# Two-layer transformer on one core: output normalisation of the second layer's attention once per batch instead of once per head group, room for a causal constant copied by ACT, and a new list of steps

## The reference

```python
A1 = where(causal, einsum('bhnd,bhmd->bhnm', Q1, K1) * scaling, -inf)
A2 = where(causal, einsum('bhnd,bhmd->bhnm', Q2, K2) * scaling, -inf)
attn = softmax(A1) - lam * softmax(A2)
O = einsum('bhnm,bhmd->bhnd', attn, V)
rms = sqrt(mean(O * O, axis=-1, keepdims=True) + EPS)
O = O / rms * rms_scale * (1.0 - LAMBDA_INIT)
```

## Time and profile before

| | |
|---|---|
| three runs, median | 509.58 us (508.74 to 510.84) |
| profiled execution | 509.87 us |
| its span | 507.8 us, 8609 instructions |
| PE busy | 462.9 us, 91% |
| DVE busy | 431.2 us, 85% |
| ACT, POOL busy | 265.4 us, 269.0 us |
| granted PE clock, mean | 0.979 |

### The profile page before, as it was taken

The page is one execution under the profiler, slowest core; times in us unless marked ns, Lnnn a source line. Parts: engine busy times, 40 slices in busy tenths (PEclk is TensorE's granted clock), DMA queues, the critical chain, the costliest instruction groups (busy, mean ns, idle before and its releaser), DMA issues.

```text
span 507.8 us, 8609 instructions
## 1 busy us (share of the span) xinstructions
PE 462.9 (91%) x3072; PEld 220.4 (43%) x3072; DVE 431.2 (85%) x812; ACT 265.4 (52%) x416; POOL 269.0 (53%) x229
## 2 busy tenths in 40 slices
PE   3998988999889999998899999999899899999986
PEld 2755444445344434454344444454434334433332
DVE  2735677798999999889979999979999999997894
ACT  1255553353676654346566654526775475357621
POOL 6311530364562558815645654814775759357962
PEclk9999997699999999999989999999999999999998
DMA  8800246926372521023067254121555135113100
GB/s 280 318 12 1 57 131 132 176 72 170 83 132 73 112 68 44 1 71 100 0 170 151 57 86 89 39 70 43 149 132 121 25 72 132 51 41 88 43 14 28
DMA packets 49889, 46.14 MB, mean 91 GB/s; under 512 B 6360, under 2 KB 39480, under 8 KB 49208
## 3 DMA queue, kind: packets, MB, share of 16 engines
q1 hardware_dynamic: 49848, 45.61, 35.8%
HBM read 37.47 MB, written 7.60 MB: 89 GB/s over the span
## 4 chain that ended last, share of the span: by engine, by line
PE 59%; DVE 27%; issue 5%; POOL 4%; ACT 2%; DMA 1%; SPq 1%; DVEq 0%; POOLq 0%; ACTq 0%
PE bank L779 8%; PE bank L791 6%; PE bank L770 6%; PE scores L810 6%; PE bank L865 4%; DVE h L1291 4%; DVE nmax L1315 4%; DVE h L1298 3%; PE scores L705 3%; PE scores L696 3%; PE scores L720 3%; PE scores L699 3%; PE scores L744 3%; PE scores L804 2%; DVE nmaxf L1315 2%
## 5 line engine op out<-in xcount | busy, mean ns | idle before, releaser
L1107 POOL TENSOR_TENSOR gb<-gb,wb 128x512 f32<-128x512 f32 x64 | 83.6, 1307 | 99.8 <-ACT gb L1006 83.9
L1021 ACT ACTIVATE pk<-scores 128x1024 f32<-128x1024 f32 x96 | 95.7, 1023 | 49.0 <-PE scores L810 48.6
L1100 POOL TENSOR_SCALAR_AFFINE_SELECT pk<-pk 128x512 f32<-128x512 f32 (+1 forms) x96 | 83.0, 871 | 54.1 <-ACT pk L1021 53.8
L1003 ACT ACTIVATE gt<-bank,bgh 128x512 f32<-128x512 f32 (+1 forms) x68 | 46.8, 688 | 75.5 <-PE bank L770 55.9
L1315 DVE TENSOR_REDUCE nmax<-scores 128x8 f32<-128x1024 f32 x64 | 76.8, 1214 | 6.5 <-PE scores L810 6.2
L779 PE MATMUL bank<-xnt,wu 128*128 128x512 f32 x128 | 70.0, 629 | 5.4 <-DVE h L1298 5.2
L770 PE MATMUL bank<-xnt,wg 128*128 128x512 f32 x128 | 70.2, 630 | 0.5 <-DVE hs L1298 0.3
L791 PE MATMUL bank<-h,wd 128*128 128x512 f32 x128 | 68.1, 628 | 0.6 <-DVE h L1298 0.5
L1298 DVE SCALAR_TENSOR_TENSOR h<-bank,bu,h 128x512 f32<-128x512 f32 x64 | 48.1, 751 | 10.1 <-PE bank L779 8.2
L1291 DVE SCALAR_TENSOR_TENSOR h<-gt,gb 128x512 f32<-128x512 f32 x64 | 52.1, 814 | 0.4 <-POOL gb L1107 0.4
L1111 POOL TENSOR_TENSOR orms<-oms,minus_half 128x32 f32<-128x32 f32 x8 | 43.8, 5481 | 7.8 <-DVE oms L1347 7.7
(11 more groups left out here) (258 smaller groups left out, 713.0 us busy)
## 6 DMA issues: line engine op xcount, KB each, us to landing
wb<-wt_scratch SPq DMA_DIRECT2D x64, 256.0 KB, 4.1
parts_scratch<-parts SPq DMA_DIRECT2D x48, 128.0 KB, 2.4
qa<-parts_scratch SPq DMA_DIRECT2D x32, 96.0 KB
ka<-parts_scratch SPq DMA_DIRECT2D x32, 96.0 KB
qa<-parts_scratch SPq DMA_DIRECT2D x32, 64.0 KB
ka<-parts_scratch SPq DMA_DIRECT2D x32, 64.0 KB
...
```

The costliest lines, as they stand in the source:

```text
L1003: A(gt[0:rows, c % 2, :], bank[5][0:rows, :], ACT.Tanh, bias=bgh[0:rows, j:j + 1], scale=0.5).then_inc(s_gate_act, 1)
L1021: A(dst.rearrange("p (h m) q -> p m h q", m=2), pairs[pair_of(step)][:, :, :].rearrange("p m (h q) -> p m h q", q=cols), ACT.Exp, scale=SC ...
L1100: pool.affine_select(out=dst, in_=dst, compare_op=ALU.is_ge, fill=0.0, base=0, pattern=[[0, heads], [1, P]], channel_multiplier=-1).then_i ...
L1107: pw(gb[:, c % 2, :], gb[:, c % 2, :], wb[:, k % 2, j % 2, :], ALU.mult).then_inc(s_ga_done, 1)
```

## The change

There are three parts.

1. A new kind of step, `seed`: for the units in `SEEDED`, ACT copies a 128x128 tile `late_f` (0 where the key may be seen, -1e30 elsewhere) into the eight parts of the room, and PE leaves out the mask matmuls and adds onto it. POOL makes the tile at the start, with one memset and one select. In `SEEDED` is a diagonal `max` unit if the taker two before it is of a kind in `("none",)`. The list has 64 `seed` words.
2. `back` keeps only the transpose, into one of four slots of `ot`. A new step `mix`, once for each batch, does the reciprocal, the product and the sum for all four groups; -lambda goes into the reciprocals of the second softmax first. The tiles `on` and `o12` go, `osq` and `lam_in` lie in `ot`, and the semaphore `oc_done` counts batches.
3. `PROGRAM` is a new list.

```diff
+    load/0 load/1 norm0/0 scale0/0 turn0/0 keys0/0 router0/0 inner0/0 norm0/1 picks0/0 scores0/0 hidden0/0 scale0/1
...
-N_MASKS = 10
+N_MASKS = 12
...
+SEEDED = [step for n, step in enumerate(TAKERS) if step[0] == "max" and step[4] < 2 and n >= 2 and TAKERS[n - 2][0] in ("none",)]
+SEED_RANK = {step: n for n, step in enumerate(SEEDED)}
...
-                                  start=(h == 0 and not masked), stop=True, skip_group_check=True)
+                                  start=(h == 0 and not masked and not seeded), stop=True, skip_group_check=True)
...
-                if kind in RING:
+                if step in SEED_RANK:
+                    pe.wait_ge(s_seed, SEED_RANK[step] + 1)
+                elif kind in RING:
                     ring_free(pe, step)
...
-                    last = scores(pair_of(step), b, query, P, qa, ka, MROWS, GH * g, key, P, u < 2)
+                    last = scores(pair_of(step), b, query, P, qa, ka, MROWS, GH * g, key, P, u < 2 and step not in SEED_RANK, step in SEED_RANK)
...
                 elif kind == "setup":
 
+                    act.wait_ge(s_masks_ready, N_MASKS)
...
+                elif kind == "seed" and ("max", c, *rest) in SEED_RANK:
+                    unit_step = ("max", c, *rest)
+                    ring_free(act, unit_step)
+                    A(pairs[pair_of(unit_step)][:, :, :].rearrange("p m (h c) -> p (m h) c", c=P),
+                      late_f[:, :].unsqueeze(1).to_broadcast([P, GHC, P]), ACT.Copy).then_inc(s_seed, 1)
...
                     dve.wait_ge(s_pv_ps, n + 1)
-                    V.transpose(ot[:, :, :].rearrange("p n r -> p (n r)"), bank[4]).then_inc(s_o_read, 1)
-                    dve.wait_ge(s_o_read, n + 1)
-                    link(V.reciprocal(rl1[:, :], ot[:, :, DV]))
-                    if n:
-                        dve.wait_ge(s_oc_done, n)
-                    link(V.tensor_tensor(o12[:, :, :], ot[:, :, 0:DV], wide(rl1[:, :], DV), ALU.mult))
-                    dst = oc[:, 2 * b:2 * b + 2, :].rearrange("p s (n r) -> p s n r", r=QUAD)[:, g // 2, :, g % 2 * DV:g % 2 * DV + DV]
-                    V.scalar_tensor_tensor(out=dst, in0=o12[:, BLOCKS:, :], scalar=lamq[:, g:g + 1], in1=o12[:, 0:BLOCKS, :],
-                                           op0=ALU.mult, op1=ALU.add).then_inc(s_oc_done, 1)
+                    if n >= MIX:
+                        dve.wait_ge(s_oc_done, n // MIX)
+                    V.transpose(ot[:, g % MIX, :, :].rearrange("p n r -> p (n r)"), bank[4]).then_inc(s_o_read, 1)
+                elif kind == "mix":
+                    b, m = rest
+                    n = group(c, b, m * MIX) // MIX
+                    dve.wait_ge(s_o_read, (n + 1) * MIX)
+                    link(V.reciprocal(rl1[:, :, :], ot[:, :, :, DV]))
+                    second = rl1[:, :, BLOCKS:]
+                    link(V.tensor_tensor(second, second, lamq[:, m * MIX:(m + 1) * MIX].unsqueeze(2).to_broadcast([P, MIX, BLOCKS]), ALU.mult))
+                    o = ot[:, :, :, 0:DV].rearrange("p m n d -> p (m n) d")
+                    link(V.tensor_tensor(o, o, wide(rl1[:, :, :].rearrange("p m n -> p (m n)"), DV), ALU.mult))
+                    both = ot[:, :, :, 0:DV].rearrange("p m (q n) d -> p m q n d", q=2)
+                    for a in range(MIX // 2):
+                        k = slice(2 * a, 2 * a + 2)
+                        dst = oc[:, 2 * b:2 * b + 2, :].rearrange("p s (n h d) -> p s h n d", h=2, d=DV)[:, (m * MIX) // 2 + a, :, :, :]
+                        ins = V.tensor_tensor(dst, both[:, k, 0, :, :], both[:, k, 1, :, :], ALU.add)
+                    ins.then_inc(s_oc_done, 1)
...
-                    dve.wait_ge(s_oc_done, group(c, b, GROUPS))
+                    dve.wait_ge(s_oc_done, group(c, b, GROUPS) // MIX)
```

More of the change, by code:

```diff
@@ L90 @@
[L90 to L109, removed]
@@ new lines @@
+    back/0/0/2 score/0/1/0/2 fetch/1/0 seed/1/0/0/0 up/12 scores0/2 gate/14 up/13 seed/1/0/0/1 max/1/0/0/0
+    seed/1/0/1/0 values/0/0/3 back/0/0/3 max/1/0/0/1 picks0/2 weights1/1 max/1/0/0/2 wb/8 seed/1/0/1/1 gate/15
+    max/1/0/1/0 score/0/1/1/0 values/0/1/0 mix/0/0/0 score/0/1/1/1 probs0/2 down/11 score/0/1/1/2 max/1/0/1/1 down/12
+    score/0/1/2/0 norm/0/0 back/0/1/0 score/0/1/2/1 down/13 score/0/1/2/2 up/14 max/1/0/1/2 values/0/1/1 seed/1/0/2/0
+    seed/1/0/2/1 max/1/0/2/0 gate/16 back/0/1/1 max/1/0/2/1 score/0/1/3/0 down/14 up/15 score/0/1/3/1 up/16
@@ new lines @@
+    score/0/1/3/2 seed/1/0/3/0 values/0/1/2 fetch/1/1 back/0/1/2 max/1/0/2/2 down/15 seed/1/0/3/1 max/1/0/3/0
+    values/0/1/3 back/0/1/3 max/1/0/3/1 max/1/0/3/2 mix/0/1/0 gate/17 down/16 seed/1/1/0/0 norm/0/1 seed/1/1/0/1
+    hidden0/2 seed/1/1/1/0 max/1/1/0/0 seed/1/1/1/1 gate/18 max/1/1/0/1 wb/9 seed/1/1/2/0 max/1/1/0/2 up/17 hidden1/2
+    minus/1/0 turn/0/0 wb/10 turn/0/1 up/18 values1/1 gate/19 max/1/1/1/0 max/1/1/1/1 out1/0 end/0 score/1/0/0/0
+    score/1/0/0/1 gate/20 max/1/1/1/2 down/17 fin/0 score/1/0/0/2 up/19 max/1/1/2/0 seed/1/1/2/1 out0/2 wb/11 up/20
@@ new lines @@
+    score/1/1/1/0 scale0/3 back/1/0/3 gate/24 seed/2/0/1/0 down/23 mix/1/0/0 store/2 up/24 score/1/1/1/1 score/1/1/1/2
+    gate/25 values/1/1/0 score/1/1/2/0 norm/1/0 fetch/2/0 router1/2 wb/13 back/1/1/0 down/24 turn0/3 up/25 max/2/0/0/0
+    max/2/0/0/1 gate/26 keys0/3 max/2/0/0/2 seed/2/0/1/1 max/2/0/1/0 up/26 gate/27 max/2/0/1/1 score/1/1/2/1 down/25
+    values/1/1/1 turn/1/0 max/2/0/1/2 score/1/1/2/2 down/26 gate/28 back/1/1/1 up/27 values/1/1/2 seed/2/0/2/0 wb/14
+    router0/3 score/1/1/3/0 max/2/0/2/0 up/28 score/1/1/3/1 gate/29 inner0/3 wb/15 score/1/1/3/2 seed/2/0/2/1 down/27
@@ new lines @@
+    max/2/0/2/1 max/2/0/2/2 gate/30 down/28 fetch/2/1 seed/2/0/3/0 seed/2/0/3/1 seed/2/1/0/0 seed/2/1/0/1 up/29
+    scores0/3 back/1/1/2 max/2/0/3/0 up/30 gate/31 values/1/1/3 max/2/0/3/1 max/2/0/3/2 back/1/1/3 choose1/2 down/29
+    up/31 picks0/3 gate/32 probs0/3 hidden0/3 hidden1/3 minus/2/0 mix/1/1/0 norm/1/1 max/2/1/0/0 max/2/1/0/1 up/32
+    gate/33 weights1/2 max/2/1/0/2 score/2/0/0/0 down/30 up/33 down/31 wb/16 turn/1/1 seed/2/1/1/0 down/32
+    score/2/0/0/1 seed/2/1/1/1 max/2/1/1/0 seed/2/1/2/0 gate/34 down/33 max/2/1/1/1 out1/1 end/1 score/2/0/0/2
@@ new lines @@
+    max/3/0/3/0 values/2/1/1 back/2/1/1 max/3/0/3/1 score/2/1/3/0 up/45 wb/23 gate/46 max/3/0/3/2 score/2/1/3/1
+    seed/3/1/0/0 values/2/1/2 back/2/1/2 gate/47 score/2/1/3/2 seed/3/1/0/1 down/44 fetch/3/1 minus/3/0 up/46
+    max/3/1/0/0 gate/48 max/3/1/0/1 seed/3/1/1/0 down/45 up/47 weights1/3 max/3/1/0/2 max/3/1/1/0 gate/49 seed/3/1/1/1
+    up/48 values/2/1/3 score/3/0/0/0 back/2/1/3 max/3/1/1/1 wb/24 seed/3/1/2/0 wb/25 gate/50 max/3/1/1/2 down/46 up/49
+    down/47 score/3/0/0/1 score/3/0/0/2 up/50 down/48 values1/3 score/3/0/1/0 mix/2/1/0 gate/51 norm/2/1 values/3/0/0
@@ L136 @@
+    fin/3
 """)
@@ L792, in down, with scores @@
                 m.then_inc(s_acc_ps, 1)
[L794 removed]
+            def scores(pair, b, row, cols, stat, move, rows, h0, tile0, width, masked, seeded=False):
                 per = 512 // cols
```

102 lines of the change are left out of this document (53 added, 49 removed).

## The result

| | before | changed |
|---|---|---|
| median of 4 runs | 509.16 us (506.42 to 510.84) | 517.82 us (516.52 to 520.91) |
| profiled execution | 509.87 us | 520.91 us |
| its span | 507.8 us | 519.2 us |

The ratio is 1.0193, 95% interval 1.0153 to 1.0234: slower by 1.9%, where I had forecast 1.8% faster, and above my range. Where a later run is told in microseconds from its ratio, it is the ratio times 509.5.

A forecast was written before the change was run, and what follows sets the result against it. PE and DVE were taken as two nearly full engines, with PE waiting for DVE. From 509.87 us, normalisation -6.4, front -3.3 and tail +0.5 gave 500.7, set to 500.4 for the median; range 491 to 514 us.

The forecast's parts named there:

- Causal constant: Seeding of diagonal units: the empty list issues no copy, all 256 mask records stay, POOL's added work is covered: 0 us.
- Output normalisation: DVE's work per batch falls to 4.03 us, saving 20.2 us over eight; at 0.32, 6.4 us reach the end (0 to 10.1).
- Rival 3: Normalisation in one 4.03 us block at eight places leaves PE idle, costing 9.6 us: 516.4 us, chance 0.16.
- the list's middle: Reshuffled steps in the middle of the list: no term in the sum, 5 us allowed either way.
- New list at the front: Before the first score units: first maximum at 77.5 us, 5.0 us earlier; gain 3.3 us (1.7 to 5.0).
- Tail: After the last transpose: four groups' work costs 1.1 us, moved final addition gives back 0.6; together +0.5 (-0.6 to +1.9).
- Sum: Whole kernel: 509.87 - 6.4 - 3.3 + 0.5 = 500.7 us, or 500.4 from the median of three runs.

The follow-up runs named there:

- e3a: Changed kernel with seeding switched on for 37 diagonal units (37 ACT copies, 148 mask matmuls fewer on PE): 510.53 us, ratio 1.0033.
- e8: Changed kernel with all 256 mask matmuls of the max units left out and no ACT copy instead: 509.49 us, ratio 1.0028.
- e7: Changed code on the old list, with the work of mix left out but for a one-column copy (output not normalised): 500.38 us, ratio 0.9826.
- e2: Changed code on the old list, with a mix right behind the fourth back of each batch: 515.92 us, ratio 1.0114.
- e6: Changed code on the old list, with a mix for two head groups behind every second back: 513.24 us, ratio 1.0088.
- e12: Changed code on the old list, with three of the blocks and chunk 2's final addition placed by hand: 516.58 us, ratio 1.0136.
- e13: Changed code on the old list, each block cut into four steps and five norm steps moved three to six steps later: 529.06 us, ratio 1.0376.
- e9: Kernel before, code and list, with the 256 mask matmuls of the max units left out: 508.33 us, ratio 1.0012.
- e5: Changed kernel with the old list up to the first max unit and the new list's order behind it: 522.84 us, ratio 1.0282.
- e4: Changed kernel with the new list up to the first max unit and the old list with the blocks behind it: 526.0 us, ratio 1.0354.
- e1: Kernel before with the new list, its seed and mix words taken out: 536.46 us, ratio 1.0537.

## Why the prediction was wrong

**Causal constant.** Right for what is issued: 256 mask records, no line of ACT's. The remark that the list was written with the 64 words in it was right, and belonged into the sum as a term, not among the reasons for a rival: lighter diagonal units, which the seeds were to bring, are worth 8 us on this list (e3a, e8).

**Output normalisation.** DVE's saving within the group was right (20.0 us against 20.2; 32.5 left against 4.03 x 8 = 32.2), though 8.3 us turned up in the expert combination and 7.3 in the steps before `minus`, none of which the change touches. The term made of it, 6.4 us off the time, is the largest error of the sum. Its factor was wrong: 0.17 (e7) makes 3.4 us, not 6.4. The share of the chain says what an engine carries now, not what comes back when it carries less. And it had no price for the work standing in one block: on the old list the new form with its tail costs 5.8 us (e2), where -6.4 + 0.5 had been forecast, 11.7 us apart.

**Rival 3, the block,** has the total nearest to the measured one (516.4 against 517.8), in part by luck. On the old list its direction holds: 5.8 us net (e2), or 9.2 with e7's average relief of 3.4 added back, which is an estimate; I had 9.6 and no relief. But the other parts of its sum were off, by 8.6 us for the list's middle, and in the changed kernel PE waits only 7.2 us behind the blocks, where the kernel before has 3.6 at its own places. That the length of the block is the reason isn't shown (e6, e12, e13). The rival's other argument, a list laid out for lighter PE units, is the one that e3a, e8 and e9 bear out. I had given it 0.16.

**New list at the front.** The first maximum was right: 77.25 against 77.5. The gain of 4.5 us on the new list (e5) agrees with 3.3 within its noise.

**Tail.** From the last `back`'s transpose to the end it takes 20.8 us in e2 and 21.4 in the changed kernel, where it was 19.2: +1.6 and +2.2, the latter just above its end of +1.9. The path was wrong there. POOL's power, 5.80 us from 504.33, releases DVE's next step, so the moved final addition gives nothing back, while all that stands between transpose and power counts:

```profile
510.16 0.69 DVE L1389 TENSOR_TENSOR oc<-oc,orms 128x512 f32<-128x512 f32 x1 [1.10 <-POOL orms L1134]
```

**Sum.** Two steps failed. The first is the output normalisation's -6.4 us: with the tail it turned out as +5.8, not -5.9. The second is "the reshuffled middle of the list has no term; I give it 5 us either way": it costs 8.6 us (e5 less e2, about 5 us of noise either way). I took a list of 633 steps as neutral wherever no row spoke against it. Against -5.9, -3.3 and 0 stand +5.8, -4.5 and +8.6, which is the 19 us between forecast and result. These three add up to the measured 9.8 us by construction, each being the difference of two neighbouring runs, so the sum confirms nothing, and the split holds only in this order: by way of e4 the front is +12.2 and the rest -8.2.

What the runs show without such a split is that the list and the length of PE's diagonal units go together. The mask records cost the new list 8.4 of the 9.8 us and the old list nothing. This kernel has the records, since its list of seeded units is empty. Part of where the rest of the new list loses can be seen: PE's wait in `minus` is 5.4 us before and 5.7 in e2, 10.2 in the changed kernel, 12.9 in e5 and 14.4 in e1, and 7.8 and 7.2 where the mask records are gone or fewer (e8, e3a). How the other microseconds spread over the single moves stays open, as does how much of e2's loss is the block's length and how much its place.
